# Attention layer of a four-layer graph network: another root, a later copy, a source factor in the projection, and another split between VectorE and ScalarE

## The reference, cut to what matters

```python
h = jnp.maximum(_layernorm(x, axis=-1), 0.0)      # (x - mean) / sqrt(var + 1e-5)
x_ = h @ weight                                   # the projection
el = x_ @ a_l                                     # destination score, one per node
er = x_ @ a_r                                     # source score, one per node
attn = jnp.exp(jax.nn.leaky_relu(el[:, None] + er[None, :], negative_slope=0.2))
attn = jnp.where(adj != 0, attn, 0.0)
denom = jnp.maximum(attn.sum(axis=-1, keepdims=True), 1e-12)
x = x + (attn / denom) @ x_ + b
```

## Time and profile before

| what | before |
|---|---|
| time, median of 3 runs (lowest, highest) | 2116.53 us (2115.51, 2118.55) |
| time of the profiled execution | 2119.51 us |
| span of the profiled execution | 2117.7 us, 1.8 us less than its time |
| attention layer: first and last masking start | 631.7 us, 911.8 us |
| mean granted TensorE clock | 0.983 of full speed |

### The profile page before, as it was taken

The page is one execution under the profiler, slowest core; times in us unless marked ns, Lnnn a source line. Parts: engine busy times, 40 slices in busy tenths (PEclk is TensorE's granted clock), DMA queues, the critical chain, the costliest instruction groups (busy, mean ns, idle before and its releaser), DMA issues.

```text
span 2117.7 us, 22055 instructions
## 1 busy us (share of the span) xinstructions
PE 1883.4 (89%) x7997; PEld 1199.4 (57%) x7997; DVE 1680.8 (79%) x2502; ACT 1466.5 (69%) x1541; POOL 0.8 (0%) x7
## 2 busy tenths in 40 slices
PE   2335999799988989889999989899999999999997
PEld 1224888578878888865555556544444444444443
DVE  4668989698878889887878853598889888988985
ACT  3445666456668989887878630498878788887873
POOL 0000000000000000000000000000000000000000
PEclk9999999899999999999999999999999999999999
DMA  9999898578875766658989778533232333323320
GB/s 388 429 428 369 334 343 337 195 282 317 318 296 199 253 241 231 241 213 329 333 329 354 300 294 300 172 114 122 94 127 102 112 104 110 119 101 127 103 76 11
DMA packets 81563, 489.51 MB, mean 231 GB/s; under 512 B 8449, under 2 KB 12546, under 8 KB 36402
## 3 DMA queue, kind: packets, MB, share of 16 engines
q1 hardware_dynamic: 77138, 485.94, 62.2%
q10 hardware_dynamic: 4320, 2.20, 0.4%
HBM read 452.36 MB, written 35.75 MB: 230 GB/s over the span
## 4 chain that ended last, share of the span: by engine, by line
PE 42%; DVE 8%; ACT 1%; issue 1%; DMA 0%; DVEq 0%; ACTq 0%
PE bank L1729 25%; PE bank L1691 5%; DVE work L1375 3%; PE bank L1605 2%; DVE reg L1375 1%; PE bank L1610 1%; PE bank L1611 1%; PE bank L1612 1%; PE bank L1634 1%; PE bank L1635 1%; DVE work L1353 1%; PE bank L1711 1%; PE bank L1598 1%; PE bank L1637 1%; PE bank L1636 1%
## 5 line engine op out<-in xcount | busy, mean ns | idle before, releaser
L1729 PE MATMUL bank<-work,reg 128*128 128x512 f32 x960 | 421.9, 595 | 17.3 <-DVE ring L1324 11.4
L1375 DVE TENSOR_TENSOR work<-work,ring 128x1536 f32<-128x1536 f32 x160 | 280.2, 1751 | 68.2 <-ACT work L784 67.4
L1729 PEld LDWEIGHTS bank<-work,reg 128*128 128x128 f32 x960 | 181.7, 191 | 245.8 <-issue 219.0
L962 DVE TENSOR_TENSOR a_lo<-ring,a_hi 128x2048 fp32r<-128x2048 f32 x128 | 290.8, 2287 | 31.4 <-ACT a_hi L553 30.5
L553 ACT ACTIVATE a_hi<-ring 128x2048 fp32r<-128x2048 f32 x128 | 244.3, 1913 | 76.1 <-PE bank L1533 76.1
L1565 PE MATMUL bank<-reg,ring 128*128 128x129 f32 x2048 | 244.8, 281 | 36.9 <-DVE ring L1076 36.8
L1565 PEld LDWEIGHTS bank<-reg,ring 128*128 128x128 f32 x2048 | 238.6, 197 | 42.4 <-DVE ring L1076 32.5
L784 ACT ACTIVATE work<-work 128x1536 f32<-128x1536 f32 x160 | 235.3, 1471 | 26.1 <-DVE work L1353 26.1
L1729 PE MATMUL bank<-reg 128*128 128x512 f32 x576 | 252.7, 592 | 0.0
L1531 PE MATMUL bank<-a_hi,s_hi 128*128 128x512 f32 x512 | 207.4, 405 | 20.1 <-DVE a_lo L962 20.1
L1533 PE MATMUL bank<-a_hi,s_lo 128*128 128x512 f32 x512 | 201.9, 394 | 0.0
(11 more groups left out here) (232 smaller groups left out, 2680.7 us busy)
## 6 DMA issues: line engine op xcount, KB each, us to landing
ring<-in_adj_units SPq DMA_DIRECT2D x320, 1024.0 KB, 4.9
ring<-in_adj_rows SPq DMA_DIRECT2D x32, 2048.0 KB, 17.0
ring<-masks SPq DMA_DIRECT2D x64, 512.0 KB, 4.6
masks<-work SPq DMA_DIRECT2D x48, 512.0 KB, 9.0
masks<-ring SPq DMA_DIRECT2D x16, 512.0 KB, 8.2
reg<-lines SPq DMA_DIRECT2D x8, 768.0 KB, 10.0
ring<-lines SPq DMA_DIRECT2D x8, 768.0 KB, 8.0
out<-ring ACTq DMA_DIRECT2D x8, 256.0 KB, 2.3
```

The source lines that it names most:

```text
L962: dve.tensor_tensor(a_lo[:, ring_at(p, g)], ring[:, ring_at(p, g)], a_hi[:, (g % 4) * UNIT:(g % 4 + 1) * UNIT].bitcast(F32), ALU.subtract) ...
L1375: dve.tensor_tensor(tv, tv, spread(ring[:, ring_at("out", g, q * W, W)], HEADS, 1), ALU.mult).then_inc(s_y, 1)
L1729: last = pe.matmul(bank[1 + k][:, :], h, tiles(c * T + t)[:, k * W:(k + 1) * W], start=t == 0, stop=t == T - 1)
```

## The change

Four things change in the attention layer.

1. `root` for "gat" is no longer a square root on ScalarE and a reciprocal on VectorE. It is a logarithm and then an exponential of -0.5 times it, both on ScalarE; the second waits on a semaphore for the first. VectorE's reciprocal is left out there, so the layer norm has 10 counted steps instead of 11.
2. `store_hT` moves on ScalarE from g = 3 to g = 5, TensorE's `project` from after g = 3 to after g = 4, and VectorE's `gat_project` from g = 5 to g = 7.
3. The factor exp(0.2 er) of the source leaves the weights. `exponentials` makes it per source (`ew02`), and GpSimd multiplies it into the projection `xw`, ones column included, in eight instructions of 128 x 516 elements, each when its part of the projection and its scores are there. TensorE's first round waits for these (`s_xscale`) in place of ScalarE's copies. The weights become exp(relu(0.8 el + 0.8 er)) for all four tiles, so one ScalarE exponential of 2048 elements without a bias takes the place of three.
4. VectorE makes one tile in even units and two in odd ones (`by_dve`), ScalarE the rest. ScalarE's exponential waits both for VectorE's maximum and for ScalarE's own relus of the same unit.

The diff, with blank lines and most of the context left out:

```diff
-LN_STEPS = {"deg": 5, "agg0": 6, "agg1": 6, "gat": 11}
+LN_STEPS = {"deg": 5, "agg0": 6, "agg1": 6, "gat": 10}
 LN_ROOT = {"deg": 3, "agg0": 4, "agg1": 4, "gat": 9}
...
         el02 = sb("el02", [P, T])
-        er02 = sb("er02", [P, T])
+        ew02 = sb("ew02", [P, T])
         er08 = sb("er08", [P, T])
...
+        def by_dve(n):
+            return 2 if n % 2 else 1
         def gat_acc(c, i):
...
         s_scale = {p: sem(f"{p}_scale_steps") for p in ("agg0", "agg1")}
+        s_log = sem("gat_norm_log")
         s_bnstat = sem("bn_statistics")
...
         s_e02 = sem("gat_exponentials")
+        s_xone, s_xscale = sem("gat_ones_column"), sem("gat_projection_scaled")
         s_gmax, s_grelu, s_gexp, s_gy = sem("gat_max"), sem("gat_relu"), sem("gat_exp"), sem("gat_weights")
...
+            pool.wait_ge(s_xone, 1)
+            for g in range(G):
+                pool.wait_ge(s_pkeep_act, g + 1)
+                pool.wait_ge(s_e02, 3 if g < EARLY // Q else 6)
+                block_xw = xw[:, g * Q:(g + 1) * Q, :]
+                pool.tensor_tensor(block_xw, block_xw,
+                                   ew02[:, g * Q:(g + 1) * Q].unsqueeze(2).to_broadcast([P, Q, P + 1]),
+                                   ALU.mult).then_inc(s_xscale, 1)
...
                 act.wait_ge(s_ln[p], c * LN_STEPS[p] + LN_ROOT[p])
-                act.activation(rstd[:, Q:2 * Q], rstd[:, 0:Q], ACT.Sqrt).then_inc(s_root[p], 1)
+                if p == "gat":
+                    act.activation(rstd[:, Q:2 * Q], rstd[:, 0:Q], ACT.Ln).then_inc(s_log, 1)
+                    act.wait_ge(s_log, c + 1)
+                    act.activation(rstd[:, 2 * Q:3 * Q], rstd[:, Q:2 * Q], ACT.Exp, scale=-0.5).then_inc(s_root[p], 1)
+                else:
+                    act.activation(rstd[:, Q:2 * Q], rstd[:, 0:Q], ACT.Sqrt).then_inc(s_root[p], 1)
...
                 act.activation(el02[:, tiles_], v[:, 0, :], ACT.Exp, scale=SLOPE).then_inc(s_e02, 1)
-                act.activation(er02[:, tiles_], v[:, 1, :], ACT.Copy, scale=SLOPE).then_inc(s_e02, 1)
+                act.activation(ew02[:, tiles_], v[:, 1, :], ACT.Exp, scale=SLOPE).then_inc(s_e02, 1)
                 act.activation(er08[:, tiles_], v[:, 1, :], ACT.Copy, scale=1 - SLOPE).then_inc(s_e02, 1)
...
                         keep_h(c - 1)
-                    if c > 1 and g == 3:
+                    if c > 1 and g == 5:
                         store_hT(c - 1)
...
                         act.wait_ge(s_mm["agg1"], G * C - 3 + n)
-                    for q in (2, 3):
+                    for q in range(by_dve(n), Q):
                         m = g * Q + q
-                        act.activation(gunit(n)[:, q * W:(q + 1) * W], reg4[:, at(c, W, 0, W)], ACT.Relu,
-                                       bias=er08[:, m:m + 1]).then_inc(s_grelu, 1)
+                        last = act.activation(gunit(n)[:, q * W:(q + 1) * W], reg4[:, at(c, W, 0, W)], ACT.Relu,
+                                              bias=er08[:, m:m + 1])
+                    last.then_inc(s_grelu, 1)
                     act.wait_ge(s_gmax, n + 1)
-                    act.activation(gunit(n)[:, 0:2 * W], gunit(n)[:, 0:2 * W], ACT.Exp).then_inc(s_gexp, 1)
-                    act.wait_ge(s_grelu, 2 * (n + 1))
-                    for q in (2, 3):
-                        m, y = g * Q + q, gunit(n)[:, q * W:(q + 1) * W]
-                        act.activation(y, y, ACT.Exp, bias=er02[:, m:m + 1]).then_inc(s_gexp, 1)
+                    act.wait_ge(s_grelu, n + 1)
+                    act.activation(gunit(n), gunit(n), ACT.Exp).then_inc(s_gexp, 1)
             def sign_of(n):
...
                 dve.wait_ge(s_root[p], cc)
-                s.link(dve.reciprocal(rstd[:, 2 * Q:3 * Q], rstd[:, Q:2 * Q]))
+                if p != "gat":
+                    s.link(dve.reciprocal(rstd[:, 2 * Q:3 * Q], rstd[:, Q:2 * Q]))
                 for q in range(Q):
...
                     if p == "agg1" and c == 1:
-                        dve.memset(xw[:, :, P:P + 1], 1.0)
+                        dve.memset(xw[:, :, P:P + 1], 1.0).then_inc(s_xone, 1)
                     for g in range(G):
...
                     dve.wait_ge(s_mm["agg1"], G * C - 3 + n)
-                for q in (0, 1):
+                for q in range(by_dve(n)):
                     m = g * Q + q
                     last = dve.tensor_scalar(gunit(n)[:, q * W:(q + 1) * W], reg4[:, at(c, W, 0, W)],
-                                             elr[:, 2 * m + 1:2 * m + 2], er02[:, m:m + 1], ALU.add, ALU.max)
+                                             er08[:, m:m + 1], 0.0, ALU.add, ALU.max)
                 last.then_inc(s_gmax, 1)
...
                         gat_nodes_out(c, s)
-                    if c > 1 and g == 5:
+                    if c > 1 and g == 7:
                         gat_project(c - 1)
                     dve.wait_ge(*loaded("gat", c, g))
-                    dve.wait_ge(s_gexp, 3 * (n + 1))
+                    dve.wait_ge(s_gexp, n + 1)
                     y = ring[:, ring_at("gat", g)]
...
                     if c == 0:
-                        pe.wait_ge(s_pkeep_act, g + 1)
+                        pe.wait_ge(s_xscale, g + 1)
                     pe.wait_ge(s_gy, n + 1)
...
                         turn_h("gat", c - 1)
-                    if c > 1 and g == 3:
+                    if c > 1 and g == 4:
                         project("gat", c - 1)
```

## The result

| | median | lowest, highest | runs |
|---|---|---|---|
| before | 2116.53 us | 2115.51, 2118.55 | 5 |
| changed | 2103.62 us | 2101.93, 2107.76 | 5 |

The ratio is 0.9941, with a 95% interval of 0.9929 to 0.9953: 12.9 us faster, where 27.2 were forecast. The profiled execution took 2101.93 us (span 2100.1). The gain is a little under half of what was said. The time lies within the stated range of 2084 to 2107, near the end that the rival with the table loads gave it.

A forecast was written before the change was run, and what follows sets the result against it. ScalarE was taken to set the 35.5 us round (31.2 busy, 4.3 waiting). Gains 3.1 (first round), 22.5 (five rounds to 31.0), 3.4 (last piece), less 1.5 and 0.3, made 27.2: 2089.3 us, range 2084 to 2107.

The forecast's parts named there:

- the rival with the table loads: Attention root on ScalarE: logarithm and exponential still cost two table loads a round; round 33.5 us, time 2106.3, chance 0.16.
- What bounds the kernel: Attention layer rounds of 35.5 us: ScalarE sets the round, 31.2 busy plus 4.3 waiting; TensorE and VectorE wait in turn.
- the root: ScalarE's square root replaced: two table loads, 2.57 us a round, go if one set serves; the logarithm adds about 0.3.
- The copy at g = 5: ScalarE's copy of transposed features, moved later: its 4.3 us wait goes, and a hole of up to 1.7 us opens.
- the hole behind the node update: ScalarE idle before unit 4's exponential, waiting for VectorE's maximum delayed by its node update: up to 1.7 us, about 1.4.
- ScalarE's other terms: Per round on ScalarE: relus 12.2 us, merged exponentials 14.6, hand-overs 1.6 (0.2 each), node copies 1.0.
- the rival that ends slower: ScalarE's exponential waits behind its own relus; slower from 0.75 us a hand-over, 2130 us at 1.0; chance 0.06.
- TensorE's clock: Rival: after a wait TensorE's matmuls run 1.7 us longer; round 32.1 us, gain about 21.5, time 2095, chance 0.12.
- the two engines' hindering: GpSimd's eight scalings and VectorE slowing each other: bounded by 0 and 9.6 us, taken as 0.
- The start: Ten ScalarE units ahead of the first node update go from 3.39 to 3.55 us each, losing 1.5 us.

The follow-up runs named there:

- part 3 alone: Kernel before with only the source factor on GpSimd and one merged exponential per unit; 2110.16 us beside 2119.95, ratio 0.9958.

## Why the prediction was half right

**What bounds the kernel: right as a sum, not as a price list.** ScalarE's 31.2 us busy and its wait of 4.3 fill the round, and taking part 2 out of the changed kernel gave back the whole gain. But 4.3 us less of waiting alone made a round 0.3 shorter, and 2.2 less of work alone 0.8.

**The failed step: the root.** The prediction had "two table loads, 2.57, go if logarithm, exponential, relu and copy can stay in one set", gave the case 0.62 and its failure 0.16. They can, but they did not: the loads that were placed do not use the common set. Logarithm and exponential have one load each in every round, and with the set loaded by name none. That condition was worth 2.7 us in a round and 18.6 us in the layer. With it met, the layer is 29.7 us shorter than before and the first round 30.2 long, where the forecast had 27.2 and 30.3; so the rest of the sum was right in total, with errors that partly cancel (below). The rival "the table loads stay" had a round of 33.5 and 2106.3 us; measured were 33.4 to 33.7 and 2103.6. The Trainium skill (ScalarE: Activation LUTs, "Table sets: the hidden batching unit") says one set holds both functions and a pair needs one load; the run with the named set agrees on the first, with no load in seven rounds, and the changed kernel disagrees on the second, with 14. The sentence spoke for the forecast, but the trace of before showed only a load at each change between square root and exponential, and nothing of which set would be taken for a logarithm.

**The copy at g = 5: right in the whole, wrong as a term by itself.** In the changed kernel the copy's idle time is 0 and the hole behind the node update 1.20 (1.4 forecast). But the 4.3 us do not "go": alone the edit gave 1.3 us in the layer, since a hole of 3.3 opened that the old wait had covered. The forecast's size rested on ScalarE's shorter sum as well.

**ScalarE's other terms: right.** Relu 0.61 a tile, exponential 1.91 with a pitch of 1.82, hand-over 0.10 plus lost overlap 0.10. So the rival that ends slower, which decided at a hand-over of 0.75 us, had nothing to it. That "part 3 and 4 together make ScalarE 1.2 slower in a round" is about what came, by these terms. Yet part 3 alone gained 6.4 us of the layer, because the wait for the transposes took up only part of it.

**VectorE: over-costed.** A tile's pitch is 0.40, not 0.45 (one pointer operand and an immediate instead of two pointers; 0.88 a pair), and VectorE was busy 29.1 a round, not 30.1.

**TensorE's clock: seen, and hidden.** TensorE in order of time in the changed kernel:

```profile
749.63 10.99 PE L1585 MATMUL bank<-reg,ring 128*128 128x129 f32 x96 [2.17 <-DVE ring L1096]
...
783.33 10.99 PE L1585 MATMUL bank<-reg,ring 128*128 128x129 f32 x96 [2.44 <-DVE ring L1096]
...
816.74 12.60 PE L1585 MATMUL bank<-reg,ring 128*128 128x129 f32 x96 [2.16 <-DVE ring L1096]
```

A gap of 2.2 to 2.4 us stands in each of these rounds. Behind two of the three the 96 matmuls took 10.99, behind the third 12.60, in a round whose mean granted clock was 0.95; the rounds, 33.4 to 33.7, did not follow, since ScalarE set them. With the set named the clock is 1.00 in all seven stretches, so the rival did not come there either.

**GpSimd: the size right, the two engines' hindering left out of the sum, and hidden.** Five of the eight took 1.05 to 1.23 us, against 1.2 at most, and one 1.39. The other two took 3.10 and 2.86, beside VectorE's instructions that grew longer in the same stretches. So (8.47 + 4.05) / 8 = 1.6 us is a mean of two kinds and the size of neither; the eight took 12.5 together, where the prediction's bound was 9.6.

**The start:** the first node update came at 677.5 instead of 676.3; 1.2 us lost, 1.5 forecast.

## What to carry to other kernels

A change that replaces one function by two on ScalarE is worth its table loads, and whether those go is decided by which set is loaded, not by which sets exist: count the loads per function in the profile after, and name the set when two functions share one. A wait inside a cycle of three engines has a price only together with what it covers: take the engine's timeline, remove the wait, and ask what the engine would stand for next; here it was 3.3 of 4.3 us. And name the conditions that a forecast's largest term hangs on: here one line of code decided 18.6 us of the layer. When the sums of three engines lie within a microsecond of each other, the order of single instructions decides; one maximum moved ahead of a node update brought more than the exchange of whole tiles.

## What the runs showed of the hardware that was not expected

VectorE and GpSimd slow each other by whole instructions: four small VectorE steps took 3.88 us instead of 1.12, one masking 3.01 instead of 2.29, and two of GpSimd's multiplications 3.10 and 2.86 where the shortest took 1.05. The Trainium skill (SBUF — State Buffer, "SBUF: two separate sides") says that GpSimd and some VectorE instructions, those with two inputs in SBUF among them, hold a shared port pair exclusively, so that the other waits for the whole instruction. These rows agree with it: GpSimd's 2.86 us from 656.02 are about one of its short ones on top of the 1.96 for which the masking of 655.69 still ran. The price in the kernel's time could not be measured. A table load takes 1.283 us every time, and the activation behind it starts at once: 785.63 + 1.28 = 786.91, next start 786.93. The stage behind the layer, untouched by any of these edits, took 276.7 us in the changed kernel and 283.6 before (first to last low part, 915.3 to 1192.0 and 926.5 to 1210.1). In twelve other profiles it lies between 276.6 and 283.5, without following the edits. It follows the mean granted clock of the stage: 0.97 in the three longest (283.4 to 283.6), 0.98 in three of 279.8 to 280.9, and 0.99 in the other eight, 276.6 to 279.6. TensorE is the fullest engine there, busy 272.1 of 276.7 us in the changed kernel. Why the clock differs from run to run stays open. This stage is why the layer's own length, and not the whole time, was used to compare single parts.
